# Attention before a mixture of experts: GpSimd adds a fifth pair of exponential blocks, and the residual's bias adds move behind the first two groups' low halves

## The reference

```
scores = einsum('bhqd,bhkd->bhqk', Q, K) / sqrt(32)      # 16 heads of 32; Q from layernorm(x), K and V from ctx
attn   = softmax(scores, axis=-1)
out    = einsum('bhqk,bhkd->bhqd', attn, V)
x = x + tanh(g_xattn) * (out @ Wo.T + bo)
x = x + tanh(g_ffn) * moe(layernorm(x))                  # 8 experts, top 2, fixed capacity
```

## Time and profile before

| | |
|---|---|
| median of 3 runs | 1780.01 us (1779.67 to 1781.52) |
| profiled execution | 1780.2 us |
| its span | 1778.5 us |
| PE busy | 1695.5 us (95%) |
| DVE, ACT, POOL busy | 60%, 45%, 31% |
| one batch of attention, from output projection to output projection | 104.40 us |

### The profile page before, as it was taken

One profiled execution on the slowest core, in us unless ns is written; L12 is line 12 of the kernel. 1 busy time (PEld: TensorE's weight loads), 2 busy tenths in 40 slices (PEclk: granted clock), 3 DMA queues, 4 the chain that ended last, 5 costly groups with the idle time before them and its releaser, 6 DMA issues.

```text
span 1778.5 us, 29096 instructions
## 1 busy us (share of the span) xinstructions
PE 1695.5 (95%) x10109; PEld 827.1 (47%) x10109; DVE 1061.4 (60%) x2100; ACT 800.1 (45%) x1094; POOL 554.7 (31%) x524
## 2 busy tenths in 40 slices
PE   7999999999999999999729999999999999999997
PEld 4324243342424334242307556574655657465563
DVE  6768867787886868768686536253453625334331
ACT  4563736546373654636315335161533516144340
POOL 2353635536363553626210212112111211211101
PEclk9999999999999999999859999999999999999999
DMA  6334263444426343432213734526262452626302
GB/s 223 115 65 147 76 175 110 115 136 91 146 80 162 121 109 124 97 101 90 111 41 101 196 87 128 134 100 164 73 176 70 132 132 100 163 71 176 71 32 29
DMA packets 214606, 203.17 MB, mean 114 GB/s; under 512 B 121812, under 2 KB 162912, under 8 KB 210456
## 3 DMA queue, kind: packets, MB, share of 16 engines
q1 hardware_dynamic: 193432, 181.80, 33.8%
q0 software_dynamic: 21120, 20.67, 6.6%
HBM read 134.57 MB, written 43.63 MB: 100 GB/s over the span
## 4 chain that ended last, share of the span: by engine, by line
PE 85%; DVE 9%; issue 2%; POOL 2%; DMA 1%; ACT 1%; SPq 0%; DVEq 0%; ACTq 0%; POOLq 0%
PE psum L1713 23%; PE psum L1661 22%; PE psum L1434 8%; PE psum L1463 6%; PE psum L1444 5%; PE psum L1478 5%; PE psum L1454 5%; PE psum L1561 5%; PE psum L1489 4%; DVE mx L1051 4%; POOL pt L638 1%; DVE reached L1176 1%; DVE stats L936 1%; PE psum L1406 0%; DVE wT L971 0%
## 5 line engine op out<-in xcount | busy, mean ns | idle before, releaser
L1713 PE MATMUL psum<-w,hT 128*128 128x512 f16 (+1 forms) x1920 | 415.7, 379 | 0.0
L1661 PE MATMUL psum<-xgT,w 128*128 128x308 f16 (+1 forms) x3072 | 408.4, 293 | 0.8 <-DVE xgT L1276 0.8
L1051 DVE TENSOR_REDUCE mx<-psum 128x1 f32<-128x512 f32 x512 | 327.9, 686 | 99.0 <-PE psum L1444 96.7
L1661 PEld LDWEIGHTS psum<-xgT,w 128*128 128x128 f16 x3072 | 296.2, 97 | 109.3 <-DVE xgT L1276 1.0
L1713 PEld LDWEIGHTS psum<-w,hT 128*128 128x128 f16 (+1 forms) x1920 | 199.2, 104 | 213.8
L910 ACT ACTIVATE h<-psum,b1c 128x308 f32<-128x308 f32 (+1 forms) x256 | 118.2, 512 | 341.5 <-PE psum L1661 337.7
L715 POOL DMA_INDIRECT out_dram<-y,idx_now x40 | 89.4, 2235 | 478.8 <-DVE y L1340 307.0
L1299 DVE TENSOR_TENSOR hT<-h,hT 128x615 f16<-128x615 f32 x128 | 102.5, 801 | 202.7 <-ACT hT L913 202.5
L1337 DVE SCALAR_TENSOR_TENSOR y<-psum,b2b 128x512 f32<-128x512 f32 (+1 forms) x40 | 27.7, 692 | 259.7 <-PE psum L1713 259.7
L1434 PE MATMUL psum<-actT,wT 128*128 128x512 f16 x768 | 179.2, 381 | 2.0 <-DVE wT L971 2.0
L1444 PE MATMUL psum<-stk 96*128 96x512 f16 x512 | 170.7, 383 | 9.5 <-DVE mx L1051 1.5
(11 more groups left out here) (219 smaller groups left out, 1820.4 us busy)
## 6 DMA issues: line engine op xcount, KB each, us to landing
stage<-in_L_ffn_W_dram SPq DMA_DIRECT2D x62, 1024.0 KB
stk<-qk_rows SPq DMA_DIRECT2D x192, 128.0 KB, 2.5
qk_rows<-qks SPq DMA_DIRECT2D x64, 256.0 KB, 2.5
xin<-in_x_dram SPq DMA_DIRECT2D x8, 1024.0 KB, 5.4
cin<-in_ctx_dram SPq DMA_DIRECT2D x8, 1024.0 KB, 7.7
xres<-in_x_dram SPq DMA_DIRECT2D x8, 1024.0 KB, 5.8
out_dram<-xres SPq DMA_DIRECT2D x32, 256.0 KB, 2.2
x_split<-x2hl SPq DMA_DIRECT2D x32, 256.0 KB, 2.3
```

Source lines behind the costliest of these rows:

```text
L1051: v.reduce_max(mx[:, KT * t + qt:KT * t + qt + 1], ps, AX.X).then_inc(read, 1)
L1661: mm = t_.matmul(psum[:, (2 * m + ch) % 4, 0:c1 - c0], w1[:, wp, kt, m * P:(m + 1) * P], xgT[:, KT * xp + kt, c0:c1], start=(kt == 0 and ( ...
L1713: mm = t_.matmul(psum[0:rows, Y_BANK[i], :], hT[:, hp, k, c * P:c * P + rows], w2[:, wp, k, :], start=(k == 0 and (hp, wp) == (0, 0)), sto ...
```

## The change

`PAIRS` becomes 5. The fifth pair is units 8 and 9; their separate `with_ones` in slots 17 and 18 go, and one `with_ones` for the pair stands in slot 19. `PAIR_SUM` names for each pair the unit whose buffer takes the sum: the first one (0, 2, 4, 6) for the old pairs, the second one (9) for the new pair. GpSimd's adds for the fifth pair wait for the values' product of unit 9 (slot 16), and stand where the residual's adds stood. The residual's adds go in twos behind the low halves of group 0 and group 1. ScalarE's wait for the buffer of a unit that a pair's add only reads is now for that add and not for the `with_ones`.

```diff
-PAIRS, PT_UNITS = 4, 5
-SUMS = {10: (("pair", 0),), 12: (("pair", 1),), 14: (("pair", 2),), 16: (("pair", 3),), 17: (("unit", 8),),
-        18: (("unit", 9), ("unit", 10)), 19: (("unit", 11),), 20: (("unit", 12), ("unit", 13)),
+PAIRS, PT_UNITS = 5, 5
+PAIR_SUM = (0, 2, 4, 6, 9)
+SUMS = {10: (("pair", 0),), 12: (("pair", 1),), 14: (("pair", 2),), 16: (("pair", 3),),         18: (("unit", 10),), 19: (("pair", 4), ("unit", 11)), 20: (("unit", 12), ("unit", 13)),
...
-                    pool.wait_ge(pv_done, UNITS * b + (2 * p + 1))
+                    pool.wait_ge(pv_done, UNITS * b + (PAIR_SUM[p] + 1))
                     for hf in range(2):
                         copied(pool, use, ("ST", 2 * p + 1, hf), b)
                         for j in range(2):
-                            into = pt_units[2 * p % PT_UNITS][:, hf, j, :]
-                            g.tensor_tensor(into, into, pt_units[(2 * p + 1) % PT_UNITS][:, hf, j, :],
+                            into = pt_units[PAIR_SUM[p] % PT_UNITS][:, hf, j, :]
+                            g.tensor_tensor(into, into, pt_units[(4 * p + 1 - PAIR_SUM[p]) % PT_UNITS][:, hf, j, :],
                                             ALU.add).then_inc(pair_added, 1)
 
-                pool.wait_ge(xres_in, 16 * b + 16)
-                pool.wait_ge(tgbo_ready, 1)
-                pool.wait_ge(mrow_ready, NG * b + NG)
-                for tt in range(KT):
-                    g.tensor_tensor(xres[:, tt, :], xres[:, tt, :], tgbo[:, :], ALU.add).then_inc(xres_biased, 1)
                 for gr in range(NG):
...
                     g.tensor_tensor(aT[:, 1, gr, :], a32[:, :], aT[:, 0, gr, :], ALU.subtract).then_inc(a_ready, 1)
+                    if gr < 2:
+                        if gr == 0:
+                            pool.wait_ge(xres_in, 16 * b + 16)
+                            pool.wait_ge(tgbo_ready, 1)
+                        for tt in (2 * gr, 2 * gr + 1):
+                            g.tensor_tensor(xres[:, tt, :], xres[:, tt, :], tgbo[:, :], ALU.add).then_inc(xres_biased, 1)
...
+                            elif u - PT_UNITS < 2 * PAIRS and u - PT_UNITS not in PAIR_SUM:
+                                act.wait_ge(pair_added, 4 * PAIRS * b + (4 * ((u - PT_UNITS) // 2) + 2 * hf + 2))
...
-                        src = pt_units[(2 * n if kind == "pair" else n) % PT_UNITS]
+                        src = pt_units[(PAIR_SUM[n] if kind == "pair" else n) % PT_UNITS]
```

## The result

The changed kernel takes 1782.41 us (median of 20 runs, 1780.33 to 1784.88), the kernel before 1779.57 (20 runs). The ratio is 1.0017, 95% interval 1.0011 to 1.0023: slower by some 3 us. The profiled execution took 1783.4, its span is 1781.7. I had forecast 1787.2, 7.2 us more: the direction and the place were right, and the size was more than double.

The account below looks back on a forecast made before the run. PE was taken to bound the kernel, without gaps in slots 16 to 22, and then to wait for POOL's late low half of group 2: seven batches x 1.1, batch 7 -0.6, +7.2 us: 1787.2, range 1777.5 to 1793.

Parts of the forecast that it names:

- PE waits for ScalarE in slot 18: PE loses one with_ones, 0.86 a batch, but waits 0.25 in slot 18 behind ScalarE; 0.62 is left.
- projection starts: In batch 2 the next projection could start at 332.71 instead of 333.33.
- fifth pair's adds: POOL's four new adds run from 315.1 to 321.5, one alone (1.24), three beside DVE (1.72 each).
- low half of group 2 ends: POOL's product that the projection needs ends at 335.6 in batch 2; it is wanted at 334.01.
- 7th matmul starts: The projection's 7th matmul starts at 335.75, PE waiting 1.7 for POOL, 1.1 later than before.
- the sum over POOL's chain: POOL's work from 315.1 to group 2's low half: 331.2 alone, 335.6 with DVE's turns, 336.5 at most.
- a turn: POOL's adds and DVE's two-input instructions exclude each other: 1.72 for one of each, an add alone 1.24.
- The sum over the batches: Whole kernel: seven batches lose 1.1 each, +7.8, batch 7 gains 0.6; +7.2 us.
- the transposing DMAs: Eight DMAs after DVE's c(3) and x(3) come some 2.5 to 3.3 later, at no cost.
- The clean gain: Rival: POOL's group 2 is ready by 334.0, each batch gains 0.62, giving 1775.0; chance 0.12.
- the first rival: The gain comes through: 0.62 a batch, 1775.0, or 1773.1 if slot 17's wait vanishes too; chance 0.12.
- The draw: Rival: POOL and DVE pack better, 7th matmul at 334.5 to 335.0, 1778.7 to 1782.2; chance 0.14.

Follow-up runs that it names:

- e11: The changed kernel run again, on one chip with repeats of two other kernels: median 1782.80 us, ratio 1.0019 to the kernel before.
- e12: Changed kernel with VectorE's seven input splits replaced by transposes of the high half (output not the reference's): 1774.51 us, ratio 0.9975 to the kernel before.
- e5: Changed kernel with one product with ones in each of slots 17 to 19: 1783.30 us, ratio 1.0018 to the kernel before.
- e4: Changed kernel with the residual's adds back in their old place, between the last pair and group 0: 1816.30 us, ratio 1.0224 to the kernel before.
- e1: Changed kernel with all four residual adds moved behind group 2's low half: 1773.06 us, ratio 0.9967 to the kernel before.
- e2: Changed kernel with VectorE's seven input splits replaced by float16 copies of the input (output not the reference's): 1773.04 us, ratio 0.9979 to the kernel before.
- e8: Residual's adds in their old place with the fifth pair, ScalarE's high half of group 1 in slot 20, not 19: 1795.67 us, ratio 1.0094 to before.

## Why the prediction was off

Each step, in batch 2; the changed kernel's times less 1.12, by which its unit 9 starts later.

| step | forecast | measured |
|---|---|---|
| PE waits for ScalarE in slot 18 | 0.25 | 0.24 (1.28 for 1.04) |
| projection starts | 332.71 | 332.85 |
| fifth pair's adds | 315.1 to 321.5 | 315.13 to 321.46 |
| low half of group 0 ends | 324.3 | 324.33 |
| residual adds 1, 2 end | 327.8 | 327.24 |
| low half of group 1 ends | 330.6 | 330.44 |
| residual adds 3, 4 end | 333.6 | 333.36 |
| low half of group 2 ends | 335.6 | 335.27 |
| 7th matmul starts | 335.75 | 335.32 |
| a batch against before | +1.1 | +0.7 |

**The step that failed is the sum over POOL's chain, from the fifth pair's adds to the 7th matmul: each term is in it and some were mis-sized, first of all residual adds 1 and 2.** I charged them a turn each, 3.44; they took 2.95, since the first was issued 0.01 ahead of t(1), and only the second lost a turn. With the gap that I had put ahead of them that is 0.56 too much. Behind them a32 and low half of group 1 went the other way: 1.64 and 1.48 for my 1.52 and 1.17, and only 0.16 of the 0.56 was left. Residual adds 3 and 4 and group 2's own two instructions came 0.08 and 0.09 shorter than charged, which makes 0.33 at the low half's end. And I charged 0.15 from there to the matmul, for the semaphore and a weight load that nothing hides; no row of the kernel before that I showed has that term, and it was 0.05. Together 0.43 a batch. That it isn't more is luck, since the second error hid most of the first. The terms are small against a chain of 20 us, but what counted was the chain less the 19.5 that it could take before anything was lost, so an error of 2% in the chain became one of 40% in the loss of 1.1.

**The sum over the batches.** Batches 1 to 6 lose 0.71 each for my 1.12, which takes 2.5 from the forecast of 7.2. I gave batch 0 the same loss; its 7th matmul starts at 126.17 and started at 124.53 + 1.30 = 125.83, so it loses 0.3, and 0.8 go. Batch 7 was to gain 0.6. It did gain 0.56 in its tail, and waited 0.59 longer for a DMA of the stacked heads in slot 0 (1.40 for 0.81), which I hadn't looked at, so 0.7 come back. That makes, but for rounding, the 4.7 at the last projection. The longer DMA wait can't be laid on the change: in its second profile (e11) the same kernel waits 0.90 there. The rest of the difference to the forecast came behind the attention, in a stretch that scatters by more.

**What held.** The stretch without a gap on PE; ScalarE's part of the gain; the turns as the cause (e12); the place, and the engine that ends the wait (7 waits, all by the low half's line); no wait in batch 7; the transposing DMAs, which start 2.9 later (329.61 less 1.12, for 325.62) at no cost. Not foreseen: the 0.18 in slot 21, where ScalarE's high half of group 1 waits for the late t(1) ahead of unit 14's exponential. I had priced that neighbour of the chain at nothing. In the changed kernel the wait at the projection swallows it, and in e5 it takes up the 0.24 that PE gains ahead of it; in e4, where t(1) ends 3.8 later than in the changed kernel, it makes, with the lower clock behind it, 2.8 of the 4.95 us that a batch loses.

**The rivals.** The clean gain was real and 3 us of GpSimd's work away: e1 has 103.79 a batch, -0.62, which is the first rival's number. The fifth pair was worth having; the residual's second half stood in the wrong place. The draw came close: the 7th matmul starts at 335.32, nearer to its 334.5 to 335.0 than to my 335.75, and 1782.4 is next to its upper end, 1782.2. But PE did wait for group 2's low half, in batches 0 to 6, and its plain gain did not come through.

**The turns.** "SBUF — State Buffer" of the Trainium skill, section "Who interferes with whom", says that VectorE's instructions with two SBUF inputs and GpSimd's reads exclude each other, and that copies and casts can do so in a double-port mode; e12's undelayed transposes and e2's copies, 0.41 alone and 1.50 beside GpSimd, agree. It also says that whoever issues first holds the ports; t(1), issued 0.01 behind and then 1.80 long for 0.69, agrees.

## What to carry to other kernels

Work moved from a full engine to an idle one is paid in deadlines, not in busy time: find the latest moment at which the receiving engine must have its next product ready, and put what has no deadline (here the residual's adds, which VectorE first needs at 343.78, 7 us behind the matmul that waited for the low half) behind it. With engines that run in order, follow each delayed result one consumer further: an instruction that waits on it holds up everything queued behind it, as ScalarE's high half held up the exponentials. Where two engines share ports, count the other one's instructions in the stretch, and give a difference of two long chains the error of the chains.

## What the runs showed of the hardware

- A transposing VectorE instruction is free beside GpSimd's adds (0.62 each in e12), a cast from float32 to float16 is not (1.50 for 0.41 in e2), although both have one SBUF input.
- After a gap of 3.4 us PE ran its products at 1.93 for 1.07 and the granted clock of the next 6.7 us was 0.75 (e4). The same followed a gap of 2.1 us in e4's batch 7: a product with ones of 1.95 for 1.04, the granted clock 0.51 from 888.2 to 891.7. Gaps of 1.0 us in the changed kernel, and of 1.6 and 0.8 in e8, left rows behind them at their usual 1.06.
- GpSimd's a32, a one-input instruction, let a second VectorE instruction go first each time that it met two in a row (1.53 and 1.64 for 0.69); none of its adds did in these rows.
